# Second half of a gated FFN: seven block products for eight, and each unit's down product inside the next unit

## The chip, the cores and the metric

One NeuronCore of a Trainium2 chip runs the whole program. The metric is the device time of one execution in microseconds, from launch to end. A profile of one execution comes with it: its span runs from the first to the last instruction.

## The reference

```
xn  = layernorm(x)                                 # x: 8 batches of 512 rows, 512 wide
s   = selective_scan_block(xn)                     # 512 wide
h   = rmsnorm(xn) * ln2
mod = 0.1 * tanh(attention(rmsnorm(xn) * ln1) @ A)
gate = silu(h @ W_in.T + mod * (h @ A) @ B)        # 2048 wide
up   = h @ W_up.T                                  # 2048 wide
out  = x + s * silu(xn + (gate * up) @ W_down.T)
```

All of it is float32. The change concerns the last four lines for gate and up columns 1024 to 2047.

## The kernel before, in words

The kernel runs the scan block, then attention (both untouched), then the FFN. A float32 product is made of float32r parts: each operand is split into a high and a low part, and `project3` (L69 to 75) issues three matmuls for each 128 of the inner dimension: high by high, high by low, low by high. A matmul has a 128x128 weight and 512 columns.

The FFN (from L2021) goes over the hidden width in two halves of 1024. A *column* q is one batch b and one slice f of 128 hidden units: q = 64 half + 8 b + f. For it TensorE makes the gate (4 inner steps x 3 = 12 matmuls, plus one of the modulation, L2200) in bank PS0 or PS1 and the up product (12) in PS2 or PS3. ScalarE makes silu of the gate into SG, VectorE multiplies by up (L2293), ScalarE rounds it to the high part GH, VectorE subtracts for the low part GL (L2295). The *down* product of column q - 1 follows column q: 4 row tiles x 3 matmuls (L2224 to L2226), summed over eight columns in PS4 to PS7. The lines L72 to L74 of the profile are the three matmuls of `project3`.

At the end of a batch's eight columns the first half copies the four banks to M1 (L2304) and SP stores them in the scratch m. In the second half SP fetches x, s and m ("fetched"), GpSimd makes xn from x and adds m (L2329, L2332), VectorE adds the banks (L2275), ScalarE takes silu, VectorE multiplies by s and adds x, and SP stores the output ("written"). The very last batch has its own ending, L2231 to L2236.

Weights come in slices of 128 hidden units: SP loads gate, up and down slices in STG3, VectorE scales them (L2282), ScalarE rounds, VectorE subtracts (L2284). Slices 8 to 15 are converted while the last batch of the first half runs. The rows of batch b, split in high and low, lie in the scratches rh and rl; SP loads them in FH and FL.

The order is one list, `ffn_order`, of pairs (kind, number). Every engine walks the whole list and acts on the kinds it knows, in that order, so an instruction of an engine waits for all that the list has before it on this engine. SP's DMAs all go through one queue. Engines are tied by semaphores (`wait_ge`, `then_inc`).

Of the kernel before, what the change touches and what calls it, by code (L numbers as in the profile page):

```python
# [24 lines left out]
def f32(ap):  # L25
    return ap.bitcast(F32)
# [6 lines left out]
def build(nc, x, WinT, convw, convb, WxT, Alog, dtb, outWT, Dp, ln1, ln2, WqT, WkT, Wv, Wo, Aw, Bw, WgT, WuT, WdT,  # L33
          ident, umask, arow, maskt, maskT, out):
    ctx = ExitStack()
    with ctx:
# [1988 lines left out]
        m_dn, m_fn, m_xn, m_w, m_ws = sems("m_dn m_fn m_xn m_w m_ws")  # L2025
# [9 lines left out]
        XN = [sb(re_, "XN0", [128, DM])]  # L2035
# [8 lines left out]
        ST = [sb(re_, f"ST{i}", [128, DM]) for i in range(4)]  # L2044
        M1 = [sb(re_, f"M1{i}", [128, DM]) for i in range(4)]
        XN.append(sb(re_, "XN1", [128, DM]))
        re_.close()
        wd_ = WdT.rearrange("(f p) m -> f p m", p=128)

        LAST = 16 * NB - 1  # L2050

        def ffn_order():


            yield "slice", 4
            yield "sums", 4 * NB - 1
            yield "slice", 5
            yield "rows", 1
            yield "down", 0
            yield "down", 1  # L2060
            yield "down", 2
            yield "column", 4
            yield "modulation", NB - 1
            yield "product", 4
            yield "slice", 6
            yield "down", 3
            for half in range(2):
                for b in range(NB):
                    for f in range(8):
                        q = 64 * half + 8 * b + f  # L2070
                        if q > EARLY:
                            yield "column", q
                            yield "product", q

                            if (f or b) and q < LAST - 1:
                                yield "down", q - 1
                        if f == 0 and b and (half == 0 or b + 1 < NB) or q == 64:
                            yield "rows", 8 * half + b + 1
                        if half == 1 and 1 <= f <= 4 and b > 0:
                            yield "written", 4 * (b - 1) + f - 1  # L2080
                        if q == EARLY + 1:
                            yield "slice", 7
                        if half == 1 and f == 5:
                            yield "fetched", b
                        if half == 0 and b == NB - 1 and f > 0:
                            yield "slice", 7 + f
                if half == 0:
                    yield "down", 63
                    yield "slice", 15
            yield "ended", LAST  # L2090
            for step in range(5):
                if step < 4:
                    yield "drained", 4 * (NB - 1) + step
                if step:
                    yield "written", 4 * (NB - 1) + step - 1
# [37 lines left out]
        def ffn_sync(sp):  # L2133
# [7 lines left out]
            for kind, n in work:  # L2141
                if kind == "slice":
                    load_slice(sp, n)
                elif kind == "rows":
# [5 lines left out]
                    load_rows(sp, n)  # L2150
                elif kind == "down" and n % 8 == 7:
                    h = n // 8
                    if h < NB:
                        for u in range(4):
                            sp.wait_ge(m_fn, 4 * h + u + 1)
                            sp.dma_start(mn_[4 * h + u], M1[u][:, :]).then_inc(m_m[u], 16)
                elif kind == "fetched":
                    for u in range(4):
                        if n == 0:
                            sp.wait_ge(m_m[u], 16 * NB)  # L2160
                        else:
# [12 lines left out]
            for u in range(4):
                sp.wait_ge(m_t[u], 64 * NB)

        def ffn_tensor(pe):
            for kind, q in work:
# [49 lines left out]
                elif kind == "ended":  # L2228
                    def down(k, q, stop=False):
                        c, f, g = slice(128 * k, 128 * k + 128), q % 8, q % 4  # L2230
                        pe.matmul(PS[4 + k][:, :], GH[g][:, c], DW[:, f, 0, :], start=False, stop=False, skip_group_check=True)  # L2231
                        pe.matmul(PS[4 + k][:, :], GH[g][:, c], DW[:, f, 1, :], start=False, stop=False, skip_group_check=True)
                        return pe.matmul(PS[4 + k][:, :], GL[g][:, c], DW[:, f, 0, :], start=False, stop=stop, skip_group_check=True)

                    pe.wait_ge(m_gl, q)
                    for k in range(4):  # L2236
                        down(k, q - 1)
                    pe.wait_ge(m_gl, q + 1)
                    for k in range(4):
                        down(k, q - 2)  # L2240
                        down(k, q, stop=True).then_inc(m_dn, 1)
                elif kind == "modulation":
                    pe.wait_ge(a_mx, 512)
                    attn_tensor(pe, [("modulation", q, None)])

        def ffn_scalar(act):
            for kind, q in work:
# [19 lines left out]
                elif kind == "written":  # L2267
                    act.wait_ge(m_fn, 4 * NB + q + 1)
                    act.activation(M1[q % 4][:, :], M1[q % 4][:, :], ACT.Silu).then_inc(m_ws, 1)

        def ffn_vector(dve):
            def drain(n):
                u = n % 4
                dve.wait_ge(m_xn, 2 * n + 2)
                dve.tensor_tensor(M1[u][:, :], M1[u][:, :], PS[4 + u][:, :], ALU.add).then_inc(m_fn, 1)  # L2275

            for kind, q in work:
# [11 lines left out]
                elif kind == "product":  # L2289
# [5 lines left out]
                    dve.tensor_tensor(GL[g][:, :], SG[u][:, :], f32(GH[g][:, :]), ALU.subtract).then_inc(m_gl, 1)  # L2295
                elif kind == "down" and q % 8 == 7:
# [3 lines left out]
                    for u in range(4):  # L2300
                        if h < 8:
                            if h:
                                dve.wait_ge(m_m[u], 16 * h)
                            dve.tensor_copy(M1[u][:, :], PS[4 + u][:, :]).then_inc(m_fn, 1)  # L2304
                        else:
                            drain(4 * (h - NB) + u)
                elif kind == "drained":

                    dve.wait_ge(m_dn, LAST - 2 + q % 4 + 1)
                    drain(q)  # L2310
                elif kind == "written":
                    u = q % 4
# [122 lines left out]
```

## Time and profile before

| | us |
|---|---|
| three runs | 2509.97, 2514.41, 2515.86 (median 2514.41) |
| profiled execution | 2514.75, span 2511.9 |
| TensorE busy in the span | 2441.7 (97%) |
| VectorE, ScalarE, GpSimd busy | 1361.7, 1046.7, 468.0 |
| first half of the FFN, columns 5 to 63 | about 1454 to 1957 |
| second half, column 64 to the last matmul | 1957.0 to 2504.1 |

How to read it: times of the trace are from the span's start. Busy time of TensorE is not its peak, since matmuls overlap: one lasts 0.39 us and the next starts 0.23 behind it. An idle engine costs something only if the chain that ends last passes through it.

### The profile page before, as it was taken

To read this page: it belongs to the slowest core of one execution; us is meant where nothing else is said; L and a number is where in the kernel's file an instruction comes from. 1 tells how busy PE (TensorE), PEld (TensorE's weight loads), DVE (VectorE), ACT (ScalarE), POOL (GpSimd) and SP (SyncE) were. 2 spreads that over 40 slices of the span, in tenths; PEclk is the share of its full clock that TensorE was granted. 3 is DMA by queue.
4 is the path that set the end of the run, shared out by engine and by line. 5 is a ranking of instruction groups with operands and counts; after the bars stand their busy time and mean duration, and the time that the engine had idled before them with its cause. 6 is when DMAs were issued, how large, how long until landed. Compare 5 with 4: busy or idle time off the path is not lost.

```text
span 2511.9 us, 36968 instructions
## 1 busy us (share of the span) xinstructions
PE 2441.7 (97%) x14039; PEld 1979.3 (79%) x14039; DVE 1361.7 (54%) x2860; ACT 1046.7 (42%) x1791; POOL 468.0 (19%) x430
## 2 busy tenths in 40 slices
PE   7999999999999899999999899999999999999998
PEld 5878878878778677777777688888888788888887
DVE  7856657666556688888888741221214322222223
ACT  6444544544544477777777621111112111111112
POOL 4000000000001254444544500000000202222222
PEclk9999999999999999999998999999999999999999
DMA  4000000100003777666666221001114312222212
GB/s 144 18 34 1 34 21 14 34 17 18 17 17 106 206 214 204 199 196 201 195 186 194 73 88 51 33 24 45 51 51 138 113 46 101 97 101 97 101 63 84
DMA packets 107733, 228.01 MB, mean 91 GB/s; under 512 B 15360, under 2 KB 16384, under 8 KB 101392
## 3 DMA queue, kind: packets, MB, share of 16 engines
q1 hardware_dynamic: 105056, 225.31, 28.1%
q8 instruction: 113, 1.85, 0.3%
q10 hardware_dynamic: 2496, 0.29, 0.1%
q14 instruction: 68, 0.56, 0.1%
HBM read 149.77 MB, written 75.50 MB: 90 GB/s over the span
## 4 chain that ended last, share of the span: by engine, by line
PE 86%; DVE 6%; DMA 3%; issue 2%; ACT 2%; SPq 1%; POOL 0%; DVEq 0%; ACTq 0%
PE PS L72 14%; PE PS L74 13%; PE PS L73 13%; PE PS L2224 4%; PE PS L2225 4%; PE PS L2226 4%; PE PS L1748 3%; PE PS L813 2%; PE PS L812 2%; PE PS L814 2%; PE PS L1706 2%; PE PS L1725 2%; PE PS L1707 2%; PE PS L1708 2%; PE PS L798 1%
## 5 line engine op out<-in xcount | busy, mean ns | idle before, releaser
L2293 DVE TENSOR_TENSOR SG<-SG,PS 128x512 f32<-128x512 f32 x124 | 85.2, 687 | 645.6 <-PE PS L74 644.4
L74 PE MATMUL PS<-FH,GU 128*128 128x512 f32 x992 | 388.3, 391 | 0.0
L73 PE MATMUL PS<-FL,GU 128*128 128x512 f32 x992 | 387.5, 391 | 0.0
L72 PE MATMUL PS<-FH,GU 128*128 128x512 f32 x992 | 387.3, 390 | 0.0
L1912 DVE CUSTOM_DVE_ANT_0 PS<-PS,MK 128x512 f32<-128x512 f32 (+3 forms) x512 | 243.9, 501 | 70.4 <-PE PS L1725 69.4
L2263 ACT ACTIVATE SG<-PS 128x512 f32<-128x512 f32 x124 | 74.0, 597 | 467.1 <-PE PS L2200 467.1
L2329 POOL TENSOR_SCALAR XN<-XT,MEAN,RSTD 128x512 f32<-128x512 f32 x32 | 69.4, 2170 | 940.8 <-DMA M<-m_scratch 940.8
L1848 ACT ACTIVATE PF<-PS 128x512 f32<-128x512 f32 (+1 forms) x384 | 200.6, 527 | 91.3 <-PE PS L1752 61.9
L2266 ACT CAST GH<-SG 128x512 fp32r<-128x512 f32 x124 | 76.9, 620 | 351.1 <-DVE SG L2293 351.1
L73 PEld LDWEIGHTS PS<-FL,GU 128*128 128x128 f32 x992 | 186.5, 188 | 41.1
L72 PEld LDWEIGHTS PS<-FH,GU 128*128 128x128 f32 x992 | 186.6, 188 | 40.6
L74 PEld LDWEIGHTS PS<-FH,GU 128*128 128x128 f32 x992 | 186.8, 188 | 39.8
L72 PE MATMUL PS<-XH,WH 128*128 128x512 f32 x504 | 209.5, 416 | 0.0
L2224 PE MATMUL PS<-DW,GH 128*128 128x512 f32 x500 | 195.8, 392 | 4.4 <-DVE GL L2295 4.4
L74 PE MATMUL PS<-XH,WL 128*128 128x512 f32 x504 | 198.0, 393 | 0.0
L73 PE MATMUL PS<-XL,WH 128*128 128x512 f32 x504 | 197.5, 392 | 0.0
L2225 PE MATMUL PS<-DW,GH 128*128 128x512 f32 x500 | 195.5, 391 | 0.0
L2226 PE MATMUL PS<-DW,GL 128*128 128x512 f32 x500 | 195.4, 391 | 0.0
L1725 PE MATMUL PS<-KS,QS 96*128 96x512 f32 (+3 forms) x512 | 172.2, 350 | 15.9 <-DVE MX L1912 15.7
L1917 DVE TENSOR_TENSOR PL<-PF,PH 128x1024 f16<-128x1024 f32 (+1 forms) x128 | 175.6, 1372 | 4.2 <-ACT PH L1853 4.1
L1748 PE MATMUL PS<-QS,KS 97*128 97x512 f32 (+3 forms) x512 | 168.3, 370 | 0.0
L1853 ACT CAST PH<-PF 128x1280 f16<-128x1280 f32 x128 | 161.2, 1260 | 4.1
(295 smaller groups left out, 5212.8 us busy)
## 6 DMA issues: line engine op xcount, KB each, us to landing
qk_scratch<-QT SPq DMA_DIRECT2D x128, 256.0 KB, 4.6
QS<-qk_scratch SPq DMA_DIRECT2D x96, 256.0 KB, 3.9
KS<-qk_scratch SPq DMA_DIRECT2D x96, 256.0 KB, 4.0
FH<-rh_scratch SPq DMA_DIRECT2D x16, 1024.0 KB, 5.7
FL<-rl_scratch SPq DMA_DIRECT2D x16, 1024.0 KB, 7.7
XF<-in_x_dram SPq DMA_DIRECT2D x32, 256.0 KB, 4.0
s_scratch<-ZS SPq DMA_DIRECT2D x8, 1024.0 KB, 4.3
rh_scratch<-RH SPq DMA_DIRECT2D x8, 1024.0 KB, 10.2
```

What stands on the lines that cost most here:

```text
L72: pe.matmul(o, lh(k), xh(k), start=open_ and k == 0, stop=False, skip_group_check=True)
L73: pe.matmul(o, lh(k), xl(k), start=False, stop=False, skip_group_check=True)
L74: last = pe.matmul(o, ll(k), xh(k), start=False, stop=close and k == nk - 1, skip_group_check=True)
L1725: t = pe.matmul(PS[2 + a % 2][:, at:at + n], QS[0:96, h, 128 * how:n], KS[0:96, h, 0:n], start=how != 1, stop=True, skip_group_check=True)
L1748: t = pe.matmul(p[:, at:at + n], KS[0:97, h, 128 * J:128 * J + 128], QS[0:97, h, 128 * J:512], start=len(how) == 2 and at == 0, stop=len(h ...
L1848: act.activation(PE_[u][:, o:o + at], PS[4 + a % 2][:, 0:at], ACT.Exp, scale=SC).then_inc(a_ex, 1)
L1853: act.copy(PH[u][:, :], PE_[u][:, :]).then_inc(a_ph, 1)
L1912: dve.tensor_tensor_reduce(out=p, in0=p, in1=MK[:, 512 - n:512], scale=1.0, scalar=NEG, op0=ALU.add, op1=ALU.max, accum_out=MX[w % 2][:, j ...
L1917: dve.tensor_tensor(PL[u][:, 0:n], PE_[u][:, 0:n], PH[u][:, 0:n], ALU.subtract).then_inc(a_rm, 1)
L2224: pe.matmul(PS[4 + k][:, :], GH[g][:, c], DW[:, f, 0, :], start=f == 0, stop=False, skip_group_check=True)
L2225: pe.matmul(PS[4 + k][:, :], GH[g][:, c], DW[:, f, 1, :], start=False, stop=False, skip_group_check=True)
L2226: t = pe.matmul(PS[4 + k][:, :], GL[g][:, c], DW[:, f, 0, :], start=False, stop=f == 7, skip_group_check=True)
```

## The change

**Block products.** Two batches (b0, b1) by two slices (f0, f1) by two halves of the inner dimension make a 2x2 by 2x2 block product. With the weights a11, a12 (f0), a21, a22 (f1) and rows likewise, seven products of sums and differences give what eight give (the form of Winograd). A *unit* v is one pair of batches and one pair of slices: 4 pairs x 4 units = 16 units. For each unit TensorE makes seven products of gate and of up, each 2 inner steps x 3 matmuls. Partial results are taken out of the banks by ScalarE (`copy` to P1, U2, U3, P5) between products that go on summing in the same bank, and combined by VectorE from SBUF and bank and by GpSimd (U3 += P5).

**Jobs in the first half.** The sums and differences of rows and weights are made once, by GpSimd, in 36 jobs during columns 8 to 61, and kept in three scratches (xt, sw, dw). A job is loaded by SP, done by GpSimd, kept by SP. The list has `job n + 1` (load; and do, for GpSimd) ahead of `job_kept n`.

**Skip.** xn is added to the partial sums in the first half: SP loads x in XT and VectorE makes xn ("skips"), and the copy of the four banks becomes an addition. In the second half nothing fetches x until a pair's end.

**Down.** A unit's down product (8 row tiles x 2 slices x 3 = 48 matmuls) is issued in the next unit, behind its fourth product (gate and up of s2). VectorE adds each bank to the partial tile MP in SBUF, unit after unit; at a pair's end silu, multiply by s, add x and the store follow, tile by tile. The slices 8 to 15, "fetched", "written", "drained" and "ended" are gone.

```diff
@@ ffn_order
             yield "rows", 1
+            yield "skips", 0
             yield "down", 0
...
+            ahead = 0
+            for q in range(EARLY + 1, 8 * NB):
+                b, f = divmod(q, 8)
+                yield "column", q
+                yield "product", q
+                yield "down", q - 1
+                if f == 0 and b + 1 < NB:
+                    yield "rows", b + 1
+                if f == 1 and b:
+                    yield "skips", b
+                if q == EARLY + 1:
+                    yield "slice", 7
+                if q >= 8 and q % 3 and ahead < len(jobs):
+                    if ahead == 0:
+                        yield "job", 0
+                    if ahead + 1 < len(jobs):
+                        yield "job", ahead + 1
+                    yield "job_kept", ahead
+                    ahead += 1
+            yield "second_half", 0
+            yield "down", 8 * NB - 1
@@ ffn_sync
+                elif kind == "skips":
+                    for u in range(4):
+                        if n:
+                            sp.wait_ge(m_fn, 4 * (n - 1) + u + 1)
+                        sp.dma_start(XT[u][:, :], xn_[4 * n + u]).then_inc(m_t[u], 16)
@@ ffn_vector
+                elif kind == "skips":
+                    for u in range(4):
+                        n = 4 * q + u
+                        dve.wait_ge(m_t[u], 16 * q + 16)
+                        dve.tensor_scalar(XT[u][:, :], XT[u][:, :], MEAN[:, n:n + 1], RSTD[:, n:n + 1],
+                                          ALU.subtract, ALU.mult).then_inc(m_xn, 1)
...
-                            dve.tensor_copy(M1[u][:, :], PS[4 + u][:, :]).then_inc(m_fn, 1)
+                        dve.tensor_tensor(M1[u][:, :], XT[u][:, :], PS[4 + u][:, :], ALU.add).then_inc(m_fn, 1)
@@ new: jobs
+        def keep_job(sp, n):
...
+            sp.wait_ge(j_op, j_op0 + job_ops(n) - 1)
+            sp.dma_start(to[0], high).then_inc(j_st[n % 2], 16)
+            sp.wait_ge(j_op, j_op0 + job_ops(n))
+            sp.dma_start(to[1], low).then_inc(j_st[n % 2], 16)
+
+        def do_job(pool, n):
...
+            if kind == "rows":
+                b11, b21, b12, b22, t1, t2, t3, t4 = (J[:, 256 * i:256 * i + 256] for i in range(8))
+                pool.tensor_tensor(J[:, 0:1024], J[:, 0:1024], J[:, 1024:2048], ALU.add).then_inc(j_op, 1)
...
+                pool.tensor_tensor(t1, b12, b11, ALU.subtract).then_inc(j_op, 1)
+                pool.tensor_tensor(t3, b22, b12, ALU.subtract).then_inc(j_op, 1)
...
+                pool.tensor_tensor(t2, b22, t1, ALU.subtract).then_inc(j_op, 1)
...
+                pool.tensor_tensor(t4, b21, t2, ALU.subtract).then_inc(j_op, 1)
...
+                pool.tensor_copy(R_[:, 0:1024], J[:, 1024:2048]).then_inc(j_op, 1)
...
+                pool.tensor_tensor(R_[:, 1024:2048], J[:, 1024:2048], J[:, 0:1024], ALU.subtract).then_inc(j_op, 1)
@@ new: SP ahead of the second half
+        def second_ahead(sp):
+            for r in range(2):
+                sp.wait_ge(j_st[r], j_st0[r] + 32 * len(range(r, len(jobs), 2)))
+            sp.wait_ge(m_u, 56)
+            for i in range(3):
+                load_block(sp, 0, i)
+            load_unit(sp, 0, None)
+            for i in range(8):
+                load_partial(sp, 0, i)
+            sp.wait_ge(m_u, 8 * NB)
+            load_block(sp, 0, 3)
+            load_block(sp, 0, 4)
+            sp.wait_ge(m_dn, 8 * NB)
+            load_block(sp, 0, 5)
+            load_block(sp, 0, 6)
+            load_unit(sp, 1, None)
@@ new: TensorE, one unit
+                product(XG, 0, a11_, 0, True).then_inc(n_pr, 1)
...
+                product(XU, 1, a11_, 0, True).then_inc(n_pr, 1)
...
+                pe.wait_ge(n_cp, 8 * v + 1)
+                product(XG, 0, s2_, 1).then_inc(n_pr, 1)
+                pe.wait_ge(n_cp, 8 * v + 2)
+                product(XU, 1, s2_, 1).then_inc(n_pr, 1)
+                if v:
+                    down(v - 1)
...
+                product(XG, 0, s3_, 2).then_inc(n_pr, 1)
...
+                product(XU, 1, s3_, 2).then_inc(n_pr, 1)
...
+                product(XG, 0, a22_, 3)
+                modulate(pe, XG, f1, b0).then_inc(n_pr, 1)
...
+                product(XU, 1, a22_, 3).then_inc(n_pr, 1)
...
+                product(ZG, 0, a12_, 4, True)
+                modulate(pe, ZG, f0, b0).then_inc(n_pr, 1)
...
+                product(ZU, 1, a12_, 4, True).then_inc(n_pr, 1)
...
+                product(WG, 0, s1_, 5, True).then_inc(n_pr, 1)
...
+                product(WU, 1, s1_, 5, True).then_inc(n_pr, 1)
...
+                modulate(pe, ZG, f1, b1, True).then_inc(n_pr, 1)
...
+                product(WG, 0, s4_, 6)
+                modulate(pe, WG, f0, b1).then_inc(n_pr, 1)
...
+                product(WU, 1, s4_, 6).then_inc(n_pr, 1)
@@ new: ScalarE, the end of a unit
+                act.wait_ge(n_pr, c + 11)
...
+                act.copy(P5[0][:, :], WG[:, :]).then_inc(n_cp, 1)
+                act.wait_ge(n_mu, 4 * v + 2)
+                act.copy(HH[:, 0, 0, 0, :], P1[0][:, :]).then_inc(n_hh, 1)
+                act.wait_ge(n_pr, c + 12)
...
+                act.copy(P5[1][:, :], WU[:, :]).then_inc(n_cp, 1)
+                act.wait_ge(n_ad, n_ad0 + 5 * v + 3)
+                act.activation(U3[0][:, :], U3[0][:, :], ACT.Silu).then_inc(n_si, 1)
+                act.wait_ge(n_mu, 4 * v + 3)
+                act.copy(HH[:, 1, 1, 0, :], U3[0][:, :]).then_inc(n_hh, 1)
+                act.wait_ge(n_ad, n_ad0 + 5 * v + 4)
+                act.activation(U2[0][:, :], U2[0][:, :], ACT.Silu).then_inc(n_si, 1)
+                act.wait_ge(n_mu, 4 * v + 4)
+                act.copy(HH[:, 0, 1, 0, :], U2[0][:, :]).then_inc(n_hh, 1)
@@ new: VectorE, the end of a unit
+                dve.tensor_tensor(HH[:, 0, 0, 1, :], P1[0][:, :], f32(HH[:, 0, 0, 0, :]), ALU.subtract).then_inc(n_hl, 1)
+                dve.wait_ge(n_pr, c + 13)
+                dve.wait_ge(n_qu, n_qu0 + 2 * v + 1)
+                dve.tensor_tensor(U3[0][:, :], U3[0][:, :], ZG[:, :], ALU.add).then_inc(n_ad, 1)
+                dve.wait_ge(n_si, 4 * v + 3)
+                dve.wait_ge(n_qu, n_qu0 + 2 * v + 2)
+                dve.tensor_tensor(U3[0][:, :], U3[0][:, :], U3[1][:, :], ALU.mult).then_inc(n_mu, 1)
+                dve.wait_ge(n_pr, c + 14)
+                dve.tensor_tensor(U2[0][:, :], U2[0][:, :], WG[:, :], ALU.add).then_inc(n_ad, 1)
+                dve.wait_ge(n_pr, c + 15)
+                dve.tensor_tensor(U2[1][:, :], U2[1][:, :], WU[:, :], ALU.add).then_inc(n_ad, 1)
+                dve.wait_ge(n_hh, 4 * v + 3)
+                dve.tensor_tensor(HH[:, 1, 1, 1, :], U3[0][:, :], f32(HH[:, 1, 1, 0, :]), ALU.subtract).then_inc(n_hl, 1)
+                dve.wait_ge(n_si, 4 * v + 4)
+                dve.wait_ge(n_ad, n_ad0 + 5 * v + 5)
+                dve.tensor_tensor(U2[0][:, :], U2[0][:, :], U2[1][:, :], ALU.mult).then_inc(n_mu, 1)
```

## Rows read from the trace of the kernel before

**Rows 1.** The page: sections 1 and 4 (busy us, share, instructions; chain by engine).

```profile
PE 2441.7 (97%) x14039; PEld 1979.3 (79%) x14039; DVE 1361.7 (54%) x2860; ACT 1046.7 (42%) x1791; POOL 468.0 (19%) x430
PE 86%; DVE 6%; DMA 3%; issue 2%; ACT 2%; SPq 1%; POOL 0%; DVEq 0%; ACTq 0%
```

**Rows 2.** Stages: length, busy us of five engines, clock, DMA share, GB/s.

```profile
1440.00:1957.00 517.00, 517.00 (x2270) 425.96 (x2269) 137.17 (x208) 93.77 (x157) 1.89 (x2) 1.00 0.17 61
1969.00:1985.00 16.00, 11.91 (x42) 9.61 (x43) 4.61 (x8) 3.96 (x7) 10.18 (x6) 0.79 0.68 262
1985.00:2503.00 518.00, 518.00 (x2273) 426.87 (x2272) 142.95 (x211) 90.90 (x153) 100.39 (x59) 1.00 0.23 82
925.00:940.00 15.00, 12.95 (x148) 9.80 (x147) 14.12 (x44) 13.49 (x25) 7.18 (x8) 1.00 0.72 195
```

**Rows 3.** TensorE in order of time around 1973 (start, us, what, idle before).

```profile
1973.09 0.80 PE L2224 MATMUL PS<-DW,GH 128*128 128x512 f32 x1 [4.38 <-DVE GL L2295]
...
1977.95 0.55 PE L2226 MATMUL PS<-DW,GL 128*128 128x512 f32 x1
1978.33 0.39 PE L72 MATMUL PS<-FH,GU 128*128 128x512 f32 x1
```

**Rows 4.** VectorE and ScalarE in order of time, one column's chain.

```profile
1970.98 0.68 DVE L2293 TENSOR_TENSOR SG<-SG,PS 128x512 f32<-128x512 f32 x1
1971.69 0.62 ACT L2266 CAST GH<-SG 128x512 fp32r<-128x512 f32 x1 [0.94 <-DVE SG L2293]
1972.22 0.59 ACT L2263 ACTIVATE SG<-PS 128x512 f32<-128x512 f32 x1
1972.34 0.69 DVE L2295 TENSOR_TENSOR GL<-SG,GH 128x512 fp32r<-128x512 f32 x1 [0.68 <-ACT GH L2266]
1972.95 0.68 DVE L2293 TENSOR_TENSOR SG<-SG,PS 128x512 f32<-128x512 f32 x1
```

**Rows 5.** VectorE and GpSimd in order of time, near the end.

```profile
2501.84 0.69 DVE L2275 TENSOR_TENSOR M<-M,PS 128x512 f32<-128x512 f32 x1 [0.67 <-PE PS L2233]
2503.21 1.29 POOL L2336 TENSOR_TENSOR M<-M,XT 128x512 f32<-128x512 f32 x1 [6.78 <-DVE M L2314]
2503.80 1.25 DVE L2314 TENSOR_TENSOR M<-M,ST 128x512 f32<-128x512 f32 x1
```

**Rows 6.** Groups of instructions by line, GpSimd's and one of VectorE's.

```profile
L673 POOL TENSOR_TENSOR WL<-ZS,WH 128x2048 fp32r<-128x2048 f32 x1 | 4.7, 4667 | 5.2 <-ACT WH L663 5.2
L1282 POOL TENSOR_TENSOR RC<-PN,PO 128x1024 f32<-128x1024 f32 x8 | 15.7, 1963 | 202.4 <-issue 105.8 <-DVE PN L1142 96.6
L1994 POOL CAST GU<-STGC 128x512 fp32r<-128x512 f32 x8 | 6.9, 860 | 0.5 <-POOL STGC L1985 0.2
...
L599 DVE TENSOR_SCALAR XF<-XF,MEAN,RSTD 128x512 f32<-128x512 f32 x32 | 15.8, 540 | 0.6 <-POOL RSTD L657 0.6
```

**Rows 7.** TensorE in order of time: down 10, one bank's last matmul, the very last.

```profile
1512.78 0.39 PE L2224 MATMUL PS<-DW,GH 128*128 128x512 f32 x1
...
2501.41 0.39 PE L2233 MATMUL PS<-DW,GL 128*128 128x512 f32 x1
...
2504.13 0.39 PE L2233 MATMUL PS<-DW,GL 128*128 128x512 f32 x1
```

**Rows 8.** SP in order of time at column 8, and tile FL's landing.

```profile
1493.76 0.46 SPq L2131 DMA_DIRECT2D FL<-rl_scratch  x1
...
DMA to landing us min/median/max: 7.7/8.2/9.1
```

**Rows 9.** DMA issues: count, KB each, median us to landing.

```profile
XT<-in_x_dram SPq DMA_DIRECT2D x32, 256.0 KB, 4.6
out_dram<-M SPq DMA_DIRECT2D x32, 256.0 KB, 2.0
STGA<-in_Wo_dram SPq DMA_DIRECT2D x1, 1024.0 KB, 5.7
STGK<-in_WkT_dram SPq DMA_DIRECT2D x1, 1024.0 KB, 12.1
```

More of the change, by code:

```diff
@@ L2043, in build @@
         XT = [sb(re_, f"XT{i}", [128, DM]) for i in range(4)]
[L2044 removed]
+        JOB = [sb(re_, "JOB0", [128, 2048], F32R)]
         M1 = [sb(re_, f"M1{i}", [128, DM]) for i in range(4)]
[L2046 removed]
+        JOB.append(sb(re_, "JOB1", [128, 2048], F32R))
         re_.close()
[L2048 to L2050 removed]
+        hs = ExitStack()
+        sb(hs, "KEPT", [128, 6536])
@@ L2052, in ffn_order @@
+        rows_jobs = [[("rows", p, k, t) for k in range(2) for t in range(2)] for p in range(PAIRS)]
+        unit_jobs = [[("weights", u, j, k) for j in range(2) for k in range(2)] + [("outward", u, 0, 0)] for u in range(UNITS)]
+        jobs = [job for u in range(UNITS) for job in rows_jobs[u] + unit_jobs[u]]
         def ffn_order():
@@ L2066, in ffn_order @@
             yield "down", 3
[L2067 to L2095, printed above, removed]
+            ahead = 0
[17 more added lines that the diff above has]
+                    ahead += 1
+            assert ahead == len(jobs)
+            yield "second_half", 0
+            yield "down", 8 * NB - 1
         work = list(ffn_order())
@@ L2227, in ffn_tensor @@
                     t.then_inc(m_dn, 1)
[L2228 to L2241, printed above, removed]
                 elif kind == "modulation":
@@ new lines, in build, with filled, load_unit @@
+        V_ = PAIRS * UNITS
+        a11_, a12_, s3_, a22_, s1_, s2_, s4_ = range(7)
+        fills, held = [], [0, 1]
+        for v in range(2, V_):
+            if held[ORDER[v] % 2] != ORDER[v]:
+                held[ORDER[v] % 2] = ORDER[v]
+                fills.append((v, ORDER[v], max(i for i in range(v) if ORDER[i] % 2 == ORDER[v] % 2)))
+        def filled(v):
+            return 16 * (1 + sum(use <= v and u % 2 == ORDER[v] % 2 for use, u, _ in fills))
+        def load_unit(sp, u, free):
+            if free is None:
+                sp.wait_ge(m_u, 60 if u == 0 else 8 * NB)
+            else:
+                sp.wait_ge(n_pr, 15 * (free + 1))
+            sp.dma_start(f32(SW[u % 2][:, :, :, :, :, :]).rearrange("p a b c d e -> p (a b c d e)"),
+                         f32(sw_d[u]).rearrange("p a b c d e -> p (a b c d e)")).then_inc(n_sw[u % 2], 16)
+            if free is None:
+                sp.wait_ge(m_dn, 58 + 2 * u)
+            else:
+                sp.wait_ge(n_dd, 8 * (free + 1))
+            sp.dma_start(f32(DW2[u % 2][:, :, :, :]).rearrange("p a b c -> p (a b c)"),
+                         f32(dw_d[u]).rearrange("p a b c -> p (a b c)")).then_inc(n_dw[u % 2], 16)
```

392 lines of the change are left out of this document (332 added, 60 removed).

## The prediction

> **What bounds the kernel now.** I read the page's head and chain first: TensorE is busy 97% of 2511.9 us and holds 86% of the chain that ended last [rows 1]. Then the stages: from 1440 on (the gated FFN) TensorE is busy through the whole of 517 and of 518 us at full clock, while VectorE is busy 27%, ScalarE 18%, GpSimd 2 us in the first half and 19% in the second [rows 2]. There a matmul removed is time removed, unless a wait appears. One matmul costs 518.0/2273 = 0.228 us [rows 2]. TensorE waits for another engine once: 4.38 us for VectorE's GL at 1973.09, VectorE having been held by the load of slice 15. The 12 matmuls behind that stop are 0.43 us apart (1973.09 to 1978.33 [rows 3]), the pace of 1.2 GHz where 0.228 is that of 2.4; the granted clock of 1969 to 1985 is 0.79 [rows 2]. The stop cost 4.38 + 5.24 - 12 x 0.228 = 6.9 us.
>
> The sum goes against the profiled execution's own 2514.75 us (span 2511.9), 0.3 above the median of the three runs.
>
> **1. Block products: a gain of 43.8 us.** Before, the second half has 64 columns of 12 gate, 12 up, 12 down and 1 modulation matmul: 64 x 37 = 2368. After, 16 units of 7 x 2 x 6 = 84 product, 48 down and 4 modulation matmuls: 16 x 136 = 2176. 192 fewer x 0.228 = 43.8; shapes are the same, so I take the same pitch.
>
> **2. The stop at 1973: a gain of 6.9 us.** Slices 8 to 15 and their conversion are gone, so VectorE isn't held there. What is late next is VectorE at column 9, item 5.
>
> **3. The seam between units: a loss of 20.4 us.** A unit is 136 matmuls = 31.0 us. Behind its last products one chain runs through four engines, and product 3 of the next unit waits for ScalarE's copy of product 1, which is queued behind that chain. Durations: VectorE 0.69, ScalarE 0.59 to 0.62 [rows 4], GpSimd's addition 1.29 [rows 5]; started behind one another without a wait, VectorE every 0.61, ScalarE every 0.53; from start to dependent start VectorE to ScalarE 0.71, ScalarE to VectorE 0.65 [rows 4]; from a bank's last matmul (2501.41 [rows 7]) to its reader (2501.84 [rows 5]) 0.43. In us from the unit's start:
> - ScalarE: P5[0] copied from 26.65 (product 11), HH 27.18, P5[1] 28.02 to 28.62 (product 12).
> - GpSimd: U3[0] 27.33 to 28.62. VectorE's low part of P1 is due at 27.83 and reads two SBUF tiles. Such an operation started at 2503.80 inside a GpSimd addition (2503.21 to 2504.50) took 1.25, ending 0.55 behind the addition [rows 5]. So it ends at 29.17, and GpSimd's U3[1] runs 29.17 to 30.45.
> - VectorE U3[0]+=ZG 29.1, ScalarE silu 29.8, VectorE multiply 30.5 (behind GpSimd), U2[0]+=WG 31.1, ScalarE silu 31.8, VectorE U2[1]+=WU 31.7, low part 32.3, multiply 32.94, ScalarE HH 33.65, and then the next unit's P1[0] 34.18 to 34.76.
> - Product 3 is due at 31.01 + 12 x 0.228 = 33.75 and starts at 34.82: a stop of 1.07.
>
> Without the hold by GpSimd it is 0.7. I take 1.07 for 12 of 15 seams. In units 4, 8 and 12 GpSimd also adds x to eight finished tiles ahead of its U3 additions; the last one follows VectorE's multiply of 28.4 and ends 29.8, which moves the chain by 1.5: 3 x 2.55. Sum 12.8 + 7.6 = 20.4 (range 13 to 36). Evictions 6 and 7 of those units come at 17.8 and 19.7, ahead of products 9 and 10 at 23.2 and 24.6: nothing. The down product's other inputs are 3 us old when it starts.
>
> Stops of a microsecond need not drop the clock: 925 to 940 has 2.05 us without TensorE at clock 1.00 [rows 2]. I take nothing.
>
> **4. Jobs on GpSimd: nothing of their own.** Additions take 1.96 for 1024 and 4.67 for 2048 columns, a cast of 512 takes 0.86 [rows 6]; for 1024 I take 2.1, between 1.96 and half of 4.67, and for 256, by 1.29 for 512 [rows 5], 0.78. A rows job (two operations of 1024, four of 256, a cast of 1024 at 1.2) is 2 x 2.1 + 4 x 0.78 + 1.2 + gaps 0.5 = 9.0; by the same prices a weights job is 6.8, an outward job 3.5: 16 x 9.0 + 16 x 6.8 + 4 x 3.5 = 267 us beside 56 columns x 8.43 = 472. GL can be held by one operation, 2.3 + 0.55; it is then 4.9 behind the up product, and TensorE wants it 5.7 behind (25 matmuls): covered. Bound, if that cover is short: 0.5 x 56 = 28.
>
> **5. The skip rows behind job 0: a loss of 13.5 us.** On SP the order at column 8 is partial stores, rows 2, load job 0, load job 1, keep job 0, and only then the loads of XT. "Keep" waits until GpSimd has done the job. On VectorE the four skip operations stand ahead of product 10, and TensorE's down 10 waits for its GL; it ran at 1512.78 [rows 7]. FL is issued at 1493.76 and lands 8.2 later, 1502.0 [rows 8]; of four loads of 1 MB issued 0.5 apart the first lands 5.7 and the fourth 12.1 behind its issue [rows 9], three MB in 6.4 + 1.5, 2.7 us each: job 0 has landed at 1504.7 and is done at 1513.7. Then the low store, XT issued 1514.2 to 1516, landing 4.6 later [rows 9]: 1520.3. The last skip operation (0.54 [rows 6]) ends 1520.9; multiply, cast and low part take 2.1 more by the steps of rows 4, with 0.8 of holding by job 1: 1523.8, so TensorE stops for 11 us. Then the low clock, as behind 1973: 2.5. At later block starts the job to keep is long done (5.3 jobs in 67.4 us), XT lands 20 behind the column and GL comes at 24.5 against 25.3: nothing, at worst 1 us x 4. Bounds of the item: 0 (SP gets past earlier) and 18 (each of job 0's steps a fifth longer).
>
> **6. Start of the second half: a loss of 2.0 us.** From its first product: the last jobs follow the partial stores of column 56 (at -57), by 7 us of GpSimd and 9 of store and load each; the last store has landed at -25.5. Then 17.3 MB (blocks, unit weights, partials) go through one queue at 2.7 us per MB: unit 0's weights land at -6, unit 1's at -25.5 + 2 + 46.7 = 23.2. Unit 1 begins at 88 matmuls = 20.1, and its seam wait of 1.07 lies inside that: 2.0. Later loads (4.7 MB per 31 us) are covered. Range 0 to 20.
>
> **7. The end: a loss of 6.8 us.** Before, 7.8 us from the last matmul (2504.13) to the span's end [rows 7]. After: eviction 8 starts 0.43 behind the last matmul, then each of eight tiles takes a multiply and a dependent addition, 0.72 + 0.61: 1.04 + 8 x 1.33 = 11.7; 0.3 for late STR loads; the last store as before, 2.6 (issue, 2.0 to landing [rows 9] and the end): 14.6.
>
> **8. Start of the FFN: a loss of 0.5 us.** Four skip operations (2.2 us) stand ahead of VectorE's last modulation step, which has 1.3 us to spare and part of whose wait the load hides. The partials' addition costs what the copy did: nothing.
>
> Sum: 43.8 + 6.9 - 20.4 - 13.5 - 2.0 - 6.8 - 0.5 = 7.5; 2514.75 - 7.5 = **2507.2**.
>
> **The rivals.**
> A. The skip loads don't hold VectorE long enough to stop TensorE. For: every other block start has slack. Against: SP's program order. 2507.2 - 13.5 = 2493.7.
> B. Each of the ten links of a seam is 0.1 longer (waits on two semaphores, SBUF holds): 2.1 x 12 + 3.6 x 3 = 36.0, 15.6 more: 2522.8; at half of it 2515.
> C. The slower side: late loads. Place: unit 1's first product, waiting for its weights. For: a lone 1 MB load takes 5.7 to land [rows 9], and the queue is shared with stores. Against: the four loads of rows 9, which kept 2.7. At 4 us per MB the weights land at 45.7: 22 more, 2529. From 3.4 us per MB on it ends above 2519.
> D. The change doesn't give what it says, because each seam's stop drops the clock like the one at 1973: 2.5 x 15 = 37 more, 2545. Against: 925 to 940.
> E. A skip operation waits out a whole GpSimd operation of job 1 (2.1 to 2.3, as the two-input one did at 2503.80): TensorE goes on at 1526, 2.2 later: 2509.4. No row shows a tensor_scalar beside GpSimd; that it takes 0.54 where a two-tile operation takes 0.69 speaks for another access to SBUF.
>
> The Trainium skill, "SBUF — State Buffer", section "SBUF: two separate sides", has E as a rule: VectorE and GpSimd share a port pair that is locked for a whole instruction, against VectorE operations in a 2-port mode too. For operations with two SBUF inputs the trace agrees (1.25 for 0.69); for tensor_scalar no run here shows it.
>
> **How the numbers follow.** Forecast 0.37 (own range 2499 to 2515), A 0.13, B 0.20, C 0.12, D 0.05, E 0.08, something not listed 0.05. A measurement tells 0.2% from no change, 5 us: 2509.4 to 2519.4 is "same". Faster: 0.65 of the forecast, A, half of E, some of the rest: 0.45. Same: most of the forecast's other part, half of B, half of E: 0.28. Slower: half of B, C, D and a little: 0.27. The range leaves out D and the far ends of the others: 2491 to 2530.
>
> **What would show it.** 13847 matmuls. TensorE's wait for ScalarE's copy at product 3 fifteen times, about 1.1 each, 2.5 in units 4, 8 and 12 to their successors. One stop near 1513 of some 11 us with slow matmuls behind it, and VectorE waiting for XT's load there. None near 1970 beyond 2 or 3 us. Wrong if the stop near 1513 is missing, if at a seam weights or blocks land last and not the copy, or if GpSimd's jobs of rows take over 10 us.

## The result, and the profile after

The changed kernel took 2523.55 us (median of 7 runs, 2518.15 to 2527.01) where the kernel before took 2514.41 beside it (7 runs, 2509.97 to 2518.35): a ratio of 1.0039, 95% interval 1.0028 to 1.0050. It is slower by 0.4%; 7.5 us less had been forecast. The profiled execution took 2522.65 us, 7.9 above that of before.

Sections 1, 4 and 5 of the page after, to be set beside [rows 1]: TensorE has the 192 matmuls fewer that were meant, yet its share of the last chain fell from 86% to 76%, while VectorE, DMA and issue grew. The group of the first term of a product says which wait is new.

```profile
PE 2404.3 (95%) x13847; PEld 1946.0 (77%) x13847; DVE 1490.3 (59%) x3007; ACT 1106.2 (44%) x1895; POOL 692.9 (27%) x667
...
PE 76%; DVE 9%; DMA 5%; issue 4%; ACT 3%; SPq 2%; POOL 1%; DVEq 0%; ACTq 0%
...
L72 PE MATMUL PS<-XB,SW 128*128 128x512 f32 x448 | 177.4, 396 | 20.1 <-ACT P L2612 20.1
```

I cut both traces at three matmuls: the last of the attention, the first of the second half, the last of all; and at the span's end.

| us | before | after | measured | forecast |
|---|---|---|---|---|
| FFN's first half | 517.9 | 539.0 | +21.1 | +14.0 |
| second half | 547.0 | 523.3 | -23.7 | -28.3 |
| behind the last matmul | 7.8 | 17.9 | +10.1 | +6.8 |

All three missed to the same side, by 7.1, 4.6 and 3.3, together 15.0 of the 15.4 us between forecast and profiled execution; the rest lies ahead of the FFN. The stages in numbers (columns as in [rows 2]):

```profile
1505.00:1540.00 35.00, 21.36 (x83) 17.05 (x82) 9.28 (x9) 2.34 (x4) 31.89 (x26) 0.76 0.64 213
1540.00:1970.00 430.00, 426.94 (x1871) 351.44 (x1870) 114.38 (x150) 61.22 (x101) 228.28 (x222) 1.00 0.59 196
1970.00:2505.00 535.00, 512.44 (x2216) 417.53 (x2214) 264.54 (x369) 170.15 (x290) 78.04 (x56) 0.99 0.49 183
```

TensorE's waits from 1438 to the end (who waits, for whom: us in total, times, longest). Before, this view has 4.4 us for GL and 0.7 for PL. Two new waits carry nearly all, and neither is for weights or blocks:

```profile
PE PS L72 <- ACT P L2612: 20.1, 15, 3.3
PE PS L2247 <- DVE GL L2298: 16.7, 3, 13.6
PE PS L1768 <- DVE PL L1917: 0.7, 1, 0.7
PE PS L1796 <- DVE TH L1953: 0.6, 1, 0.6
```

**The stop at 1514.** The trace of after in order of time, four engines, at column 9. SP issues XT's loads only behind job 0's low store (1515.02), and VectorE waits for them until 1520.14. GpSimd is by then in job 1:

```profile
1512.60 2.38 POOL L2390 TENSOR_TENSOR JOB<-JOB 128x1024 fp32r<-128x1024 f32 x1
...
1514.00 0.39 PE L74 MATMUL PS<-FH,GU 128*128 128x512 f32 x1
...
1515.02 0.55 SPq L2370 DMA_DIRECT2D xt_scratch<-JOB  x1
1515.60 2.60 SPq L2186 DMA_DIRECT2D XT<-in_x_dram  x4
...
1520.14 4.66 DVE L2303 TENSOR_SCALAR XT<-XT,MEAN,RSTD 128x512 f32<-128x512 f32 x4 [20.46 <-DMA XT<-in_x_dram]
1520.31 1.27 POOL L2388 CAST JOB<-JOB 128x1024 fp32r<-128x1024 f32 x1
...
1521.66 2.40 POOL L2390 TENSOR_TENSOR JOB<-JOB 128x1024 fp32r<-128x1024 f32 x1
...
1525.08 2.34 POOL L2379 TENSOR_TENSOR JOB<-JOB 128x1024 f32<-128x1024 f32 x1 [1.03 <-DMA JOB<-rl_scratch]
...
1526.07 1.90 DVE L2298 TENSOR_TENSOR GL<-SG,GH 128x512 fp32r<-128x512 f32 x1 [0.68 <-ACT GH L2276]
...
1528.02 0.80 PE L2247 MATMUL PS<-DW,GH 128*128 128x512 f32 x1 [13.64 <-DVE GL L2298]
...
1528.61 0.63 PE L2248 MATMUL PS<-DW,GH 128*128 128x512 f32 x1
```

The view of line 2303 gives the four skip operations (shortest, median, longest, ns), here and at the next block start, at 1593:

```profile
L2303 DVE TENSOR_SCALAR XT<-XT,MEAN,RSTD x4: 535/799/2557, 1520.1 to 1524.3; 128x512 f32<-128x512 f32 x4
L2303 DVE TENSOR_SCALAR XT<-XT,MEAN,RSTD x4: 830/1038/2341, 1593.1 to 1597.3; 128x512 f32<-128x512 f32 x4
```

They took 0.54 alone [rows 6]. An operation is called held here where its duration runs on until a GpSimd operation beside it is over. The second is held behind the cast (1.05) and the third through the whole addition (2.56, from 1521.8 to 1524.3); GL is held until 0.55 behind the addition of 1525.08. By durations that is 0.5 + 2.0 + 1.2 = 3.7 us of holding. The last of the four loads was issued at 1517.77 and landed 4.4 later, 1522.15, so without holding the four would have ended at 1522.7 and not at 1524.8: 2.1 + 1.2 = 3.3 us of it lie on TensorE's path, where 0.8 was forecast.

**A seam.** Unit 0 into unit 1, GpSimd, VectorE, ScalarE, TensorE in order of time. The links are the forecast ones: low part held by GpSimd (1.37), two additions of GpSimd, silu, multiply, HH, and only then P1[0] (line 2612) at 2002.03, on which product 3 waits:

```profile
1995.23 1.29 POOL L2739 TENSOR_TENSOR U<-U,P 128x512 f32<-128x512 f32 x1 [53.36 <-ACT P L2646]
...
1995.71 1.37 DVE L2705 TENSOR_TENSOR HH<-P,HH 128x512 fp32r<-128x512 f32 x1 [1.01 <-ACT HH L2648]
...
1996.60 1.63 POOL L2741 TENSOR_TENSOR U<-U,P 128x512 f32<-128x512 f32 x1
...
1997.00 0.67 DVE L2708 TENSOR_TENSOR U<-U,PS 128x512 f32<-128x512 f32 x1
...
1998.37 0.69 DVE L2711 TENSOR_TENSOR U<-U,U 128x512 f32<-128x512 f32 x1 [0.70 <-ACT U L2654]
...
2000.78 0.69 DVE L2720 TENSOR_TENSOR U<-U,U 128x512 f32<-128x512 f32 x1
...
2001.50 0.62 ACT L2660 CAST HH<-U 128x512 fp32r<-128x512 f32 x1 [1.17 <-DVE U L2720]
2002.03 0.58 ACT L2612 COPY P<-PS 128x512 f32<-128x512 f32 x1
...
2002.75 0.47 PE L72 MATMUL PS<-XB,SW 128*128 128x512 f32 x1 [0.88 <-ACT P L2612]
...
2124.81 1.30 POOL L2737 TENSOR_TENSOR MP<-MP,XTR 128x512 f32<-128x512 f32 x1 [3.22 <-DVE MP L2673]
2124.81 1.84 DVE L2705 TENSOR_TENSOR HH<-P,HH 128x512 fp32r<-128x512 f32 x1
...
2126.07 1.73 POOL L2739 TENSOR_TENSOR U<-U,P 128x512 f32<-128x512 f32 x1
...
2127.90 0.69 DVE L2708 TENSOR_TENSOR U<-U,PS 128x512 f32<-128x512 f32 x1 [1.25 <-POOL U L2739]
...
2133.66 0.47 PE L72 MATMUL PS<-XB,SW 128*128 128x512 f32 x1 [3.16 <-ACT P L2612]
...
2134.76 0.63 PE L73 MATMUL PS<-XB,SW 128*128 128x512 f32 x1
```

The rows from 2124.81 on are the seam behind unit 4, where GpSimd still adds x to a finished tile. The row of 1997.00 shows what is not held: this addition has one input in a bank, began inside GpSimd's of 1996.60 and took 0.67 all the same; the sixteen of its line took 0.67 to 0.69, all of them begun beside GpSimd's addition. Twelve seams stop TensorE for 1.04 us (1.27 between starts, less 0.23), three for 3.3; behind two of the three, eight matmuls run 0.43 apart.

**The end.** VectorE behind the last matmul of 2502.19, with SP's queue. The multiplies of the last four tiles wait, 3.3 us in all, for loads of XTR and STR that could be issued only when the tile four places earlier had left its buffer:

```profile
2506.96 0.50 SPq L2459 DMA_DIRECT2D XTR<-in_x_dram  x1
...
2508.85 0.69 DVE L2673 TENSOR_TENSOR MP<-MP,STR 128x512 f32<-128x512 f32 x1 [0.23 <-DMA XTR<-in_x_dram]
...
2511.82 0.69 DVE L2673 TENSOR_TENSOR MP<-MP,STR 128x512 f32<-128x512 f32 x1 [1.55 <-DMA XTR<-in_x_dram]
...
2514.57 0.69 DVE L2673 TENSOR_TENSOR MP<-MP,STR 128x512 f32<-128x512 f32 x1 [1.34 <-DMA XTR<-in_x_dram]
...
2516.16 0.69 DVE L2673 TENSOR_TENSOR MP<-MP,STR 128x512 f32<-128x512 f32 x1 [0.17 <-DMA XTR<-in_x_dram]
```

### The profile page after: what moved, and what is told of

Read it like the earlier page. It is cut to its first block, busy times and chain, and to the rows that moved or that the text cites. A ratio compares the mean times of both kernels' runs of the same rounds, so it can differ in the third digit from the quotient of the medians.

```text
span 2520.1 us, 37640 instructions
## 1 busy us (share of the span) xinstructions
PE 2404.3 (95%) x13847; PEld 1946.0 (77%) x13847; DVE 1490.3 (59%) x3007; ACT 1106.2 (44%) x1895; POOL 692.9 (27%) x667
## 4 chain that ended last, share of the span: by engine, by line
PE 76%; DVE 9%; DMA 5%; issue 4%; ACT 3%; SPq 2%; POOL 1%; DVEq 0%; ACTq 0%
PE PS L72 11%; PE PS L74 11%; PE PS L73 11%; PE PS L1748 3%; PE PS L813 2%; PE PS L812 2%; PE PS L814 2%; PE PS L2540 2%; PE PS L2541 2%; PE PS L2542 2%; PE PS L1706 2%; PE PS L2247 2%; PE PS L2249 2%; PE PS L2248 2%; PE PS L1725 2%
## 5 line engine op out<-in xcount | busy, mean ns | idle before, releaser
L2296 DVE TENSOR_TENSOR SG<-SG,PS 128x512 f32<-128x512 f32 x60 | 41.2, 686 | 267.1 <-PE PS L74 265.8
L72 PE MATMUL PS<-XB,SW 128*128 128x512 f32 x448 | 177.4, 396 | 20.1 <-ACT P L2612 20.1
L74 PE MATMUL PS<-FH,GU 128*128 128x512 f32 x480 | 188.1, 392 | 0.0
L72 PE MATMUL PS<-FH,GU 128*128 128x512 f32 x480 | 187.9, 391 | 0.0
L73 PE MATMUL PS<-FL,GU 128*128 128x512 f32 x480 | 187.8, 391 | 0.0
L74 PE MATMUL PS<-XB,SW 128*128 128x512 f32 x448 | 176.8, 395 | 0.0
L73 PE MATMUL PS<-XB,SW 128*128 128x512 f32 x448 | 176.6, 394 | 0.0
L2681 DVE TENSOR_TENSOR MP<-MP,PS 128x512 f32<-128x512 f32 x128 | 87.7, 686 | 130.9 <-PE PS L2542 130.7
L1089 DVE SCALAR_TENSOR_TENSOR XC<-PS,CW,XC 128x511 f32<-128x511 f32 (+2 forms) x192 | 143.6, 748 | 33.6 <-ACT XC L950 28.6
L2012 POOL TENSOR_TENSOR PL<-PF,PH 128x256 f16<-128x256 f32 x112 | 88.5, 791 | 194.9 <-ACT PH L1853 194.7
L2273 ACT ACTIVATE SG<-PS 128x512 f32<-128x512 f32 x60 | 35.8, 597 | 230.2 <-PE PS L2223 230.2
L2739 POOL TENSOR_TENSOR U<-U,P 128x512 f32<-128x512 f32 x16 | 21.6, 1350 | 406.8 <-ACT P L2646 406.8
L2276 ACT CAST GH<-SG 128x512 fp32r<-128x512 f32 x60 | 37.2, 620 | 205.5 <-DVE SG L2296 205.5
## 6 DMA issues: line engine op xcount, KB each, us to landing
SW<-sw_scratch SPq DMA_DIRECT2D x10, 3584.0 KB, 12.1
```

Of the source, the lines that this page charges most:

```text
L72: pe.matmul(o, lh(k), xh(k), start=open_ and k == 0, stop=False, skip_group_check=True)
L73: pe.matmul(o, lh(k), xl(k), start=False, stop=False, skip_group_check=True)
L74: last = pe.matmul(o, ll(k), xh(k), start=False, stop=close and k == nk - 1, skip_group_check=True)
L1089: dve.scalar_tensor_tensor(out=y[:, j:], in0=p[:, 0:S - j], scalar=CW[:, d, 3 - j:4 - j], in1=y[:, j:], op0=ALU.mult, op1=ALU.add).then_in ...
L2012: pool.tensor_tensor(PL[u][:, 1024:1280], PE_[u][:, 1024:1280], PH[u][:, 1024:1280], ALU.subtract).then_inc(a_rp, 1)
L2681: dve.tensor_tensor(MP[i][:, :], MP[i][:, :], DN[i % 4][:, :], ALU.add).then_inc(n_ev, 1)
```

## The experiments

Each is the changed kernel with one edit, compared with the kernel before on the same chip (2515.2 to 2515.8 us there). "First half", "second half" and "end" are the stages of the table above, in the profiled execution; "unchanged" means within 2 us. The part ahead of these stages, which no edit touches, took 1437.8 to 1442.4 us in nine of the ten profiled executions and 1448.1 in that of experiment 1, so what an edit gains is read from the stages, and the totals given are medians.

**1. XT's loads ahead of the job that they waited behind.** SP's plan gets the loads of the skip rows as a step of its own, at column 8b, ahead of the jobs; VectorE's operations stay where they were.

```
+            if f == 0 and b:
+                yield "skip_loads", b
             if f == 1 and b:
                 yield "skips", b
...
-            elif kind == "skips":
+            elif kind == "skip_loads":
```

> The changed kernel, and SP alone altered: the four loads of XT are issued behind the loads of rows and ahead of the jobs of the same column; VectorE's skip operations stay where they are. Theory (TensorE's stops at 1514, 1598 and 1802 all come from XT being issued behind a job's keep or load on SP, and the skip operations are then held by GpSimd's job): all three stops go, 13.8 + 1.7 + 1.7 us, with the 2.8 us of slow matmuls behind the first, 20 us in all, about 2503; XT lands some 17 us behind the column, and the four skip operations take about 2.2 us together in place of 4.7 to 5.0, since no job runs beside them. Rival (the order on SP is not the cause, GpSimd's jobs hold VectorE wherever XT comes): the stop at 1514 shrinks by less than half and the two small ones stay; 2513 or more.

Measured: 2503.81 us, ratio 0.9948 [0.9928, 0.9969]; first half 518.7, the others unchanged (523.5, 17.2). All three stops are gone. The same four operations, by line and in order of time, now ahead of GpSimd's first job, which starts at 1517.40:

```profile
L2306 DVE TENSOR_SCALAR XT<-XT,MEAN,RSTD x4: 546/546/548, 1512.3 to 1514.4; 128x512 f32<-128x512 f32 x4
```

So the place of the loads on SP is the cause of all 20 us of the first half: with it right, the jobs on GpSimd cost TensorE nothing, as item 4 said. And the same operations on the same shapes take 0.546 each without GpSimd and up to 2.56 beside it. (The profiled execution took 2509.33, with 8.2 us more ahead of the FFN than in the one of after.)

**2. The jobs begin one column later.**

```
-                if q >= 8 and q % 3 and ahead
+                if q >= 9 and q % 3 and ahead
```

> The changed kernel, and the jobs start at column 10 in place of column 8, so that job 0 is loaded behind the XT loads of column 9; all later block starts are as they were or have one job moved. Theory (only where a job that is not yet done must be kept ahead of XT is the stop long): the stop near 1514 and its slow matmuls go, 16.6 us, about 2506, and the stops of 1.7 us near 1598 and 1802 or their like stay. Rival (jobs beside the first columns of a batch stop TensorE in any case): a stop of over 5 us remains near 1514 to 1540.

Measured: 2511.73 us, ratio 0.9984 [0.9972, 0.9995]; first half 529.8. The stop at 1514 is gone, but three others stand at 1584.1, 1721.7 and 1791.2 (2.5, 1.8 and 3.9 us). A partial miss: 2506 was expected, and I had taken the later block starts for harmless. At 1579.7 XT's four operations take 829, 1043 and up to 2342 ns, as at 1593 above. At 1788.8, ahead of the stop of 3.9, they take 0.76 to 1.25 and GL 1.48, some 1.9 us of holding in all, and the first load had landed only 9.8 us behind its issue; the slow matmuls behind this stop cost 2.6 us more. From the wait list of this kernel:

```profile
PE PS L2247 <- DVE GL L2298: 7.7, 3, 3.7
...
PE PS L72 <- DMA SW<-sw_scratch: 0.5, 1, 0.5
```

The jobs' phase against the columns decides which block start is hit. That SP's order is needed for any of the stops is shown by experiment 1; the parts of holding and of late landing are read from durations and not taken apart by a run. The last line is new: here unit 1 waited 0.5 us for its weights.

**3. ScalarE rounds HH behind the next unit's P1[0].** The seam's last rounding moves behind the copy that product 3 waits for.

```
                 act.copy(P1[0][:, :], XG[:, :]).then_inc(n_cp, 1)
+                if v:
+                    act.wait_ge(n_mu, 4 * v)
+                    act.copy(HH[:, 0, 1, 0, :], U2[0][:, :]).then_inc(n_hh, 1)
...
-                act.wait_ge(n_mu, 4 * v + 4)
-                act.copy(HH[:, 0, 1, 0, :], U2[0][:, :]).then_inc(n_hh, 1)
```

> The changed kernel, and ScalarE alone altered: the last rounding of a unit (HH of U2) comes behind the next unit's copy of product 1 and not ahead of it. Theory (product 3 waits for ScalarE's copy only because it is queued behind the unit's chain): the twelve stops of 1.04 us go, the three of 3.3 us shrink to under 1.5 us, and the slow matmuls behind two of them (about 3 us) go: 12.5 + 6 + 3 = 21 us, about 2501. Rival (the chain through VectorE and GpSimd itself is too long, and what is late next is the rounding or the copy of product 2): the stops move to product 4 or to the down product with half their length or more, and under 8 us are gained.

Measured: 2500.71 us, ratio 0.9938 [0.9918, 0.9958]; second half 502.0, the others unchanged. The twelve stops of 1.04 are gone, the three behind units 4, 8 and 12 shrank to 1.5, with some 0.5 of slower matmuls behind each. It confirms that the stop is ScalarE's program order and not TensorE's need for HH:

```profile
PE PS L72 <- ACT P L2612: 4.0, 3, 1.3
```

**4. The down product behind the second product instead of the fourth.**

```
                 product(XU, 1, a11_, 0, True).then_inc(n_pr, 1)
+                if v:
+                    down(v - 1)
...
                 product(XU, 1, s2_, 1).then_inc(n_pr, 1)
-                if v:
-                    down(v - 1)
```

(ScalarE's copies of finished tiles move with it.)

> The changed kernel, and a unit's down product stands behind the next unit's second product in place of its fourth (48 matmuls, 10.9 us, between product 2 and product 3; ScalarE's silu of finished tiles moves with it). Theory (the seam's stops are a matter of where the cover stands): the copy of product 1 is ready 10 us before product 3 needs it, all fifteen stops go with the slow matmuls: 12.5 + 10 + 3 = 25 us, about 2497. Rival (the down product, started 2.7 us earlier, itself waits for the unit's last low part, ready 3.9 us behind the unit's end, or for its banks): stops of about a microsecond at its first or fifth row tile, half the gain or less.

Measured: 2492.68 us, ratio 0.9911 [0.9889, 0.9932], 4 below expectation; second half 496.0 = 2176 x 0.228, with no seam wait left, those of units 4, 8 and 12 included. From 1440 on TensorE waits only for GL (17.2 us in three times, the first half's stops) and once 0.7 for TH. So the 27.3 us between 523.3 and 496.0 are all the seam's, and the gain of the block products is there in full.

**5. The eighth product put back.** Twelve matmuls a unit, of no use to the result, go into the bank that product 9 writes next; everything else stays.

```
+                product(ZG, 0, s2_, 4, True)
+                product(ZG, 1, s2_, 4, True)
                 product(ZG, 0, a12_, 4, True)
                 modulate(pe, ZG, f0, b0).then_inc(n_pr, 1)
```

> The changed kernel with the eighth product's matmuls put back as dead weight: 12 more matmuls a unit (gate and up of s2 by block 4) into bank ZG just ahead of product 9, which opens the bank anew, so that nothing of the result changes. Theory (what the block products save is exactly their matmuls, at 0.228 us): 192 more matmuls, TensorE 43.8 us longer, about 2567; the stops at the seams stay 1.04 and 3.3 us. Rival (part of the saving was already lost, because the chain through ScalarE, VectorE and GpSimd sets the unit's length and a longer unit would hide it): the seams' stops shrink by a microsecond each and the kernel is under 30 us longer.

Measured: 2561.85 us, ratio 1.0191 [1.0174, 1.0208], 5 below expectation; second half 564.5, 41.1 more (38 in the medians). 192 x 0.228 = 43.8, less three seams of 2.5 for 3.3: at these three the rival was right, by 0.8 us each, and the twelve of 1.04 stayed. So what the 192 matmuls cost is their own time, and the block products give what item 1 forecast.

**6. The last tiles' loads early.** The last four s and x tiles are loaded into the memory of two blocks no longer needed, behind products 2 and 4 of the last unit.

```
...
+                            sp.dma_start(last_ends(i)[0], sn_[n]).then_inc(n_xb[i], 16)
+                            sp.dma_start(last_ends(i)[1], xn_[n]).then_inc(n_xb[i], 16)
...
```

> The changed kernel, and only the last pair's late loads moved: s and x of tiles 28 to 31 are loaded behind products 2 and 4 of the last unit into memory of blocks 0 and 1, and not behind each tile's store. Theory (of the 17.9 us behind the last matmul, 3.3 are VectorE waiting for XTR and the stores queue behind those loads): 14.6 us behind the last matmul, 3 to 4 us faster. Rival (the stores to DRAM, 4.3 us each in the median, and not the loads set the end): the last store still ends 17 us behind the last matmul, no change.

Measured: 2521.01 us, ratio 1.0024 [1.0014, 1.0034]; end 14.2 for 17.9, where item 7 had 14.6. VectorE no longer waits for a load there: the 3.3 us over the forecast were these waits.

**7. The same, and the finishes woven into the evictions.**

```
             for i in range(8):
                 evict(V_ - 1, i)
-            for i in range(8):
-                finish(V_, i)
+                if i >= 2:
+                    finish(V_, i - 2)
...
```

(The additions follow, each once its multiply is two operations old.)

> As ends_early, and VectorE's multiplications by s of the last pair stand between the evictions (two tiles behind), additions of x behind them without a multiplication right ahead of each. Theory (the end is VectorE's 16 operations behind the last eviction, 8 of them dependent): the last addition ends 7.8 us behind the last matmul, the span 10.4 behind it in place of 17.9: 7.5 us faster, about 2516. Rival (the evictions are delayed by the multiplications between them and the last down product waits for its banks): stops of TensorE in the last 11 us, gain under 5.

Measured: 2518.24 us, ratio 1.0012 [1.0001, 1.0023]; end 10.7, expected 10.4. The median fell by 5.3 us and not by 7.5; in the profiled execution the second half was 1.7 longer, because all three stops of 3.3 had slow matmuls behind them and not two. What is left over the 7.8 of before is VectorE's own work, with nothing idle between its operations.

**8. Experiments 1, 4 and 7 in one kernel.**

> Skip loads ahead of the jobs, the down product behind the second product, and the woven end, together. Theory (the three losses stand at different places and add up): 2523.6 - 19.7 - 30.9 - 7.5 = 2465.5, 49 us under the kernel before; TensorE without a stop over 0.3 us from column 5 to its last matmul. Rival (they share a part: with TensorE earlier, the second half's loads or the down product's low part come late): a new stop at the start of the second half or in the units, 2475 or more.

Measured: 2468.68 us, ratio 0.9816 [0.9803, 0.9830]; stages 518.7, 496.0 and 10.7. The three repairs add up, to 3 us (2465.5 was expected), and it is 1.8% faster than the kernel before. The stop of 0.8 us at 1454, for TH, stays. Sections 1 and 4 of its page, and then its whole list of TensorE's waits from 1440 on:

```profile
PE 2392.2 (97%) x13847; PEld 1938.2 (79%) x13847; DVE 1479.7 (60%) x3007; ACT 1107.9 (45%) x1895; POOL 691.5 (28%) x667
...
PE 84%; DVE 6%; DMA 3%; issue 3%; ACT 2%; SPq 1%; POOL 0%; DVEq 0%; ACTq 0%; POOLq 0%
```

```profile
PE PS L1796 <- DVE TH L1953: 0.7, 1, 0.7
```

## Why the prediction was wrong

The sign was wrong. The mechanisms were those forecast, at their places; the gain was right, and three of the losses were undersized, by 6.5 (item 5), 6.9 (item 3) and 3.3 (item 7), where item 6 was 2.0 too high.

- **Item 1 (-43.8)** held: the matmuls are 13847, their pitch 0.228 (experiments 4 and 5).
- **Item 2 (-6.9)** held: the stop at 1973 is gone, and nothing is late in its place there.
- **Item 5 (+13.5) failed by 6.5, at its step of holding.** SP's order and job 0's 9.0 us (1506.02 to 1514.98) were right. The stop was 13.8 us for 11, the slow matmuls behind it 2.8 for 2.5: 16.6. XT's last tile landed at 1522.15, where I had 1520.3, 1.9 more; TensorE, on the other side, reached this place 1.45 later than in [rows 7] (1514.23). The step "with 0.8 of holding by job 1" is what was mis-sized; it measured 3.3, 2.5 more (1.9 + 2.5 less 1.45 is 2.9; the stop was 2.8 longer). I had reasoned that a tensor_scalar, being shorter, reaches SBUF in another way, and spread the holding over GL alone. Rival E, to which I gave 0.08, was the case, and its price of 2.2 more was close to the 2.5 measured. The Trainium skill, "SBUF — State Buffer", section "SBUF: two separate sides", has it as a rule for VectorE operations in a 2-port mode, and the trace now agrees for tensor_scalar as well (2557 ns beside GpSimd, 546 without). The same item's "nothing, at worst 1 us x 4" at later block starts failed too: two stops of 1.7. At the next block start the last load landed at 1595.0; with 0.55 for its operation the four would have ended at 1595.6, and they ended at 1598.1: 2.5 us of holding. Loads landed later as well: SP's issue of four took 5.41 us at 1585.24, the first landed 7.8 behind its issue, and XT's median to landing is 7.2 for the 4.6 of [rows 9], here 3.2 more. The stop was 1.7, so by this estimate either alone would have been covered, and it took both. The two stops are 3.4 together. Experiment 1 takes away all of the item. Item 5 came to 20.0.
- **Item 8 (+0.5)** was 0.8 (what stays of the first half in experiment 1); **item 4 (0)** held once the loads came in time (experiment 1).
- **Item 3 (+20.4)** came to 27.3, and failed at two steps: the seams of units 4, 8 and 12, and the clock, which was put at nothing. Twelve seams were right to 0.03. The three behind units 4, 8 and 12 were 3.3 for 2.55. "Moves the chain by 1.5" was wrong by its own numbers: GpSimd's addition until 29.8 and U3[0] behind it end at 31.1, and without them 29.1, which is 2.0. The rest is VectorE holding GpSimd in its turn: U3[0] took 1.73 for 1.29. Then the clock: "I take nothing" rested on 925 to 940, whose 2.05 us without TensorE are several stops, the longest 1.0, and was applied to stops of 2.55 too. Behind two of these three stops eight matmuls ran at 0.43, some 1.6 us each, and the first matmul behind each of the 15 stops 0.08 longer. How much of the 1.04 is GpSimd's holding of the low part (1.37 for 0.69) no run took apart; its forecast share is 0.4.
- **Item 6 (+2.0)** was nothing. No unit waited for weights or blocks, and the second half without the seam is 2176 x 0.228 to the tenth. This is the one loss that I set too high, and by little: unit 1's weights landed at 1997.14, 18.3 us behind the second half's first product for the 23.2 forecast, and unit 1 began at 1998.97. In experiment 2 it waited 0.5 us for them.
- **Item 7 (+6.8)** was 10.1. The arithmetic chain of 11.7 was right (experiment 6: 14.2 for 14.6 in all). "0.3 for late STR loads" failed: 3.3. Each of these loads waits for the buffer of the tile four places earlier and shares SP's queue with the stores, which took up to 5.8 to land there, for the 2.0 of [rows 9].

Of the rivals, A and C were false: the skip stop was there, and no load of weights held a unit, with 1.8 us to spare. B, longer links, was false for twelve seams (1.04 for 1.07); of the three others it has the part that VectorE holds GpSimd. D, the clock, holds behind the stops of 3.3 and not behind those of 1.04: 3.2 us and not 37. E was true. The forecast was the small difference of a gain of 50.7 and losses of 43.2; 15.0 more on the losses turned the sign.

## What to carry to other kernels

With TensorE busy all the time, the matmuls saved gave their own time here (43.8 forecast, 41.1 by experiment 5 with three seams shorter); what decides is each place where a buffer, a load or a copy now stands behind new work in program order. List those places on every queue, the DMA issuing one first, and move the load or the down product and not the arithmetic: three such edits turned +0.4% into -1.8% here. And where a VectorE operation can fall beside a GpSimd one, price it at the GpSimd operation's whole length, a tensor_scalar too. Those with one input in a bank were not held here.

## What the runs showed of the hardware that was not expected

- A tensor_scalar of 128x512 fp32 took 0.546 us with GpSimd idle and 1.05, 2.34 and 2.56 beside GpSimd operations of 1.27, 2.18 and 2.40 us.
- VectorE's operations on 128x512 with one input in a bank were not held: the 16 of line 2708 and 14 of line 2296 began with over 0.4 us of a GpSimd operation still to come and took 0.67 to 0.69, as without it.
- The holding goes both ways: GpSimd's addition of 512 columns took 1.29 alone and 1.63 (1996.60) and 1.73 (2126.07) where it began while a VectorE operation with both inputs in SBUF was running.
- The granted clock was 0.61 from 2133.6 to 2138.0, behind a stop of 3.3 us, with matmuls 0.43 apart (the level of 1.2 GHz) for part of it; from 1998 to 2006, around a stop of 1.04, it was 1.00. Of three stops of 3.3 two had slow matmuls behind them (three of three in experiment 7), of twelve of 1.04 none. In between it went both ways: eight matmuls 0.43 apart behind a stop of 2.3 us (experiment 5, 1798.6), none behind one of 2.1 (experiment 3, 1599.9).
- SP's issue of four loads of 256 KB took 2.60 us at 1515.60 and 5.41 at 1585.24, and one of eight 13.43 at 1948.18, with more of the earlier transfers still under way in the last two. Why an issue takes longer no run took apart.
- Loads of 3.5 MB (28 KB a partition) landed 12.1 us behind their issue in the median and those of 1 MB 4.8 to 5.0; the first two of 3.5 MB, at the start of the second half with much else queued, took 17.7 and 16.8.
